# Cross attention's second half of heads is divided by its sums on POOL instead of DVE

## The reference

```python
d = Cx // H                      # 128 // 8 = 16
qh = (x @ wq.T + bq).reshape(Bx, N, H, d).transpose(0, 2, 1, 3)
kh = (memory @ wk.T + bk)...     # memory: the 154 context tokens
vh = (memory @ wv.T + bv)...
a = jax.nn.softmax(jnp.einsum('bhnd,bhmd->bhnm', qh, kh) / jnp.sqrt(jnp.float32(d)), axis=-1)
ca = jnp.einsum('bhnm,bhmd->bhnd', a, vh).transpose(0, 2, 1, 3).reshape(Bx, N, Cx)
ca = ca @ mha_out_w.T + mha_out_b
```

## Time and profile before

| | us |
|---|---|
| median of 3 runs | 882.4 |
| lowest and highest run | 880.11, 885.28 |
| the profiled execution | 884.99 |
| its span | 883.2 |
| PE busy | 727.9 |
| DVE busy | 570.5 |
| ACT busy | 534.4 |
| POOL busy | 322.5 |

### The profile page before, as it was taken

One profiled execution on the slowest core, in us unless ns is written; L12 is line 12 of the kernel. 1 busy time (PEld: TensorE's weight loads), 2 busy tenths in 40 slices (PEclk: granted clock), 3 DMA queues, 4 the chain that ended last, 5 costly groups with the idle time before them and its releaser, 6 DMA issues.

```text
span 883.2 us, 15858 instructions
## 1 busy us (share of the span) xinstructions
PE 727.9 (82%) x5368; PEld 476.9 (54%) x5368; DVE 570.5 (65%) x2212; ACT 534.4 (61%) x1345; POOL 322.5 (37%) x368
## 2 busy tenths in 40 slices
PE   5858788887878876788969789869888888879997
PEld 4535465565656745654546465545564564665443
DVE  5585856768646849658776747647567565873623
ACT  4248395684937425465696695795785845544542
POOL 4254624555341234234445425335233124412200
PEclk9598989998987977699999999999889898989999
DMA  8601010010100000202121301200212000004243
GB/s 261 192 10 34 13 43 13 13 32 13 43 13 1 1 1 1 67 16 69 37 67 37 90 19 40 75 1 20 71 26 55 18 26 30 13 13 126 72 129 91
DMA packets 37163, 41.83 MB, mean 47 GB/s; under 512 B 14346, under 2 KB 23772, under 8 KB 36956
## 3 DMA queue, kind: packets, MB, share of 16 engines
q1 hardware_dynamic: 37083, 40.83, 16.6%
HBM read 28.75 MB, written 2.62 MB: 36 GB/s over the span
## 4 chain that ended last, share of the span: by engine, by line
PE 45%; DVE 24%; ACT 18%; POOL 7%; issue 3%; DMA 1%; SPq 0%; DVEq 0%; POOLq 0%; ACTq 0%
ACT work L863 9%; PE moe_psum L624 5%; PE dve_psum L446 5%; PE act_psum L614 4%; PE act_psum L507 3%; PE dve_psum L517 3%; DVE work L1133 3%; PE act_psum L713 2%; PE act_psum L776 2%; DVE res_nrm L1111 2%; DVE stats L1101 2%; POOL rstd L1505 2%; DVE work L1156 2%; PE dve_psum L716 2%; POOL work L1522 2%
## 5 line engine op out<-in xcount | busy, mean ns | idle before, releaser
L1522 POOL TENSOR_TENSOR work<-work,rinv 128x512 f32<-128x512 f32 (+1 forms) x72 | 77.7, 1087 | 145.3 <-DVE rinv L1119 145.1
L863 ACT ACTIVATE work<-work,nbias,rnorm 128x128 f32<-128x128 f32 x256 | 122.7, 482 | 8.5 <-DVE nbias L1196 8.3
L1504 POOL TENSOR_SCALAR rstd<-mv 128x2 f32<-128x2 f32 x72 | 16.9, 235 | 161.2 <-DVE mv L1104 161.2
L446 PE MATMUL dve_psum<-wqkv,hTs 128*128 128x512 f32 x128 | 68.4, 661 | 2.0 <-ACT hTs L1010 2.0
L1562 POOL TENSOR_TENSOR hT<-hT,work 128x512 f32<-128x512 f32 x32 | 40.8, 1274 | 79.6 <-DVE work L1156 79.6
L846 ACT COPY v_loc<-act_psum 77x512 f32<-77x512 f32 (+2 forms) x72 | 41.6, 583 | 33.9 <-PE act_psum L451 16.2
L1133 DVE CUSTOM_DVE_ANT_0 work<-dve_psum,masks 128x128 f32<-128x128 f32 x256 | 58.2, 282 | 3.2 <-PE dve_psum L477 3.2
L846 ACT COPY hT<-act_psum 128x512 f32<-128x512 f32 (+1 forms) x60 | 31.2, 525 | 42.0 <-PE act_psum L507 23.0
L433 PE MATMUL act_psum<-ident,res_nrm 128*128 128x128 f32 x96 | 26.6, 372 | 36.4 <-DVE res_nrm L1111 36.3
L1505 POOL TENSOR_TENSOR rstd<-rstd,neg_half 128x2 f32<-128x2 f32 x72 | 52.3, 727 | 6.0
L1152 DVE TENSOR_TENSOR hT<-dve_psum,tab_a 128x512 f32<-128x512 f32 x32 | 22.1, 690 | 46.0 <-PE act_psum L458 29.6
(11 more groups left out here) (224 smaller groups left out, 2026.0 us busy)
## 6 DMA issues: line engine op xcount, KB each, us to landing
ahead<-cwT_dram SPq DMA_DIRECT2D x128, 64.0 KB, 2.0
v_loc<-v_loc SPq DMA_DIRECT2D x24, 256.0 KB, 3.7
kT<-cwT_dram SPq DMA_DIRECT2D x80, 64.0 KB, 2.0
qT<-cwT_dram SPq DMA_DIRECT2D x48, 64.0 KB, 2.1
wqkv<-in_wqkv_dram SPq DMA_DIRECT2D x2, 768.0 KB
res_nrm<-in_x_dram SPq DMA_DIRECT2D x4, 256.0 KB, 3.2
w_m<-in_w_m_dram SPq DMA_DIRECT2D x1, 1024.0 KB, 9.2
v_loc<-v_loc SPq DMA_DIRECT2D x8, 128.0 KB, 3.1
```

What stands on the lines that cost most here:

```text
L446: nc.tensor.matmul(bank[:], h, attn_w[:, k * INNER:(k + 1) * INNER], start=True, stop=True)\
L863: last = nc.scalar.activation(weights[:, i, :], weights[:, i, :], ACT.Exp, bias=nbias[u][:, b, i:i + 1], scale=scale_of(i), accum_out=sums ...
L1522: nc.gpsimd.tensor_tensor(some, some, by.unsqueeze(2).to_broadcast(list(some.shape)), ALU.mult).then_inc(ready[u], 1)
```

## The change

`divide` on DVE keeps the two reciprocals and loses the multiplication of the hi half, together with DVE's wait for its own reciprocals. POOL's `cross_attention_steps` calls `divide_half` a second time for each tile, for the hi half, right behind the lo half. Nothing else differs.

```diff
                     number, b = sm_cross(t), t % 2
                     invert_sums(u, number, b)
-                    dve.wait_ge(rinv_ready[u], half_done(number, 1))
-                    some = cprob[u][b][:, HALF:, :]
-                    nc.vector.tensor_tensor(some, some, rinv[u][:, b, HALF:].unsqueeze(2).to_broadcast([P, HALF, CTX]),
-                                            ALU.mult).then_inc(probs_hi_ready[u], 1)
...
                     for t in range(TILES):
                         divide_half(u, sm_cross(t), t % 2, cprob[u][t % 2], 0, probs_lo_ready)
+                        divide_half(u, sm_cross(t), t % 2, cprob[u][t % 2], 1, probs_hi_ready)
                         yield
```

## The result

| | before | after |
|---|---|---|
| median of the comparison, us (9 runs each) | 883.27 | 877.06 |
| lowest and highest run | 880.11, 888.09 | 874.60, 880.14 |
| profiled execution, its span | 884.99, 883.2 | 875.49, 873.7 |
| ratio of the times | | 0.9922, 95% interval 0.9896 to 0.9947 |

The changed kernel is faster by 0.8%, about 7 us with an interval of 4.7 to 9.2; the two medians are 6.2 apart. The forecast was 3.2. Its direction and range (873.5 to 885.0) held, and its size was about half.

The account below looks back on a forecast made before the run. The kernel was taken as a web of handovers between in-order engines, none filling the span (PE busy 82%). Gains at six chain places summed to 3.2 us, so 882.4 - 3.2 = 879.2 us, range 873.5 to 885.0.

Parts of the forecast that it names:

- The lock: Cross attention's divisions: DVE's and POOL's exclude each other on SBUF, so DVE's takes 1.85 us instead of 0.80.
- 281.52: Sample 0: DVE empties a bank earlier, so PE's 0.80 us wait ahead of line 723 goes; gain 0.80.
- the ten others: The ten of 16 DVE multiplications not on the chain: DVE has slack behind them, removal costed at nothing.
- 302.44: End of sample 0: PE starts on a hi half that now comes later; loss 0.25 us.
- 351.06 and 773.91: Samples 1 and 3: exp's bias is written earlier, though it waits under POOL's pair; gain 0.58 us each, bounds 0 and 1.07.
- 699.14 and 709.04: Sample 2: PE's wait at line 723 goes, gain 0.80 us; waits at lines 572, 1255 and 1262 go, gain 0.72.
- 761.70: Sample 3: line 1457 stands still until lo ends, then delays hi, PE losing 0.8 us; net gain taken as 0.
- The sum: Gains over the six places, 0.55 + 0.58 + 0.80 + 0.72 + 0 + 0.58 = 3.2 us.
- The whole wait goes: Rival: DVE's 1.85 us leaves the chain at all six places, or later steps tighten; 11.1 us, 871.3; chance 0.17.
- the six places: The six of 16 DVE multiplications on the chain: 281.52, 351.06, 699.14, 709.04, 761.70 and 773.91.
- Nothing is left: Rival: POOL's shadow on biases and other DVE lines, plus late hi halves, takes the gain; 881 to 882.4 us; chance 0.23.
- PE waits for hi: Rival: PE at line 572 waits 0.56 us for hi at each tile, 9.0 in all, 891.4 us; chance 0.10.

Follow-up runs that it names:

- ten: Kernel before, with the hi half moved to POOL only at the ten places not on the chain, (0, 2) included; 882.12 us, ratio 0.9997.
- six: Kernel before, with the hi half moved to POOL only at the six places where DVE's multiplication was on the chain; 876.24 us, ratio 0.9930.
- no_hi: Changed kernel with the hi half divided by nobody, PE waiting for its reciprocals alone; 874.9 us, ratio to before 0.9915.
- last_two: Kernel before, with the hi half on POOL in samples 2 and 3 only; 877.61 us, ratio 0.9952.
- first_two: Kernel before, with the hi half on POOL in samples 0 and 1 only; 875.97 us, ratio 0.9944.
- nudge: Kernel before, with DVE writing four reciprocals of sample 1's last tile four times more, same result; 887.81 against 880.74 us, ratio 1.0097.
- twice: Changed kernel with POOL multiplying the hi half twice, so that it comes later still; 884.62 us, ratio to before 1.0042.

## Why the prediction was right in direction and short in size

*The lock (right).* DVE's division took 1.85 because it stood still behind POOL. With both halves on POOL each takes 1.21, and with both on DVE 0.80.

*281.52 (right).* Forecast 0.80, measured 0.87. The wait ahead of line 723 is gone.

*291.42, one of the ten others (wrong).* "In the ten others DVE has slack behind it, and I cost its removal there at nothing." At (0, 2) it had none. The division held back the bias, ACT's exps and hT, and through them PE's transposes at 298.22. Its removal gave 1.77 us, 1.20 of them at the low clock too (ten), and none of them came from the clock alone (six). I had read the places from the chain that ended last, and there DVE's copy, which ended 0.06 later than ACT's, stood in ACT's place. This is the largest single term of the gain, and it was missing.

*302.44, the late hi half (right).* Forecast 0.25, measured 0.23 in the trace and 0.28 by no_hi. PE waited for a hi half at this one tile; two to four were forecast.

*351.06 and 773.91, the bias in POOL's shadow (right in size).* Forecast 0.58 each, measured 0.62 and 0.62. What I had assumed of where the bias gets in was not general. At 279.25, 694.20 and 768.33 it took 1.03, 1.03 and 1.14, through the start of the second division to its end. I had priced only waits up to the end of the division in front. In sample 1 such a wait at 339.29 cost 0.28.

*699.14 and 709.04 (right).* Forecast 0.80 and 0.72; measured 0.87 and 0.88 in the changed kernel, 1.74 for the sample in last_two.

*761.70 (wrong).* Forecast 0, because line 1457 would stand still behind lo and then push hi back by 0.8. It went first: with the division gone it starts straight behind the reciprocals, ahead of POOL. So lo was late, 0.44 at PE's line 572, and 0.79 by the start of line 593. With the wait at 339.29 the forecast was 1.1 us too good here. How much of the 0.79 is the late lo and how much the lower clock, at which PE transposed, is not shown.

*The sum (wrong, by two terms that were missing).* The terms of the edit come to 4.3 us against 3.2 forecast, with 1.77 at a place that had none and 1.1 lost where little was expected. The kernel gained 5.9 in the profile. The second step that failed is that the sum took every other stretch to keep its length. It did not. What is left over per stage is -0.1, +0.6, +1.4, -2.7, +0.9, -0.5, +2.0, net 1.6 for the changed kernel. That this goes with the clock and not with the moved divisions is shown for sample 3 (first_two has 2.3 us of it with before's instructions), for sample 2 (last_two has the same edits there and not the 0.9) and for the stretch from 1 to 2 (nudge has 6.3 of the other sign). In sample 1 PE's work from the transposes at 357.86 (351.01 in the changed kernel) to the end takes 5.41 us before and 4.02 after, at granted clocks of 0.64 and 0.98; that and the 0.6 between samples 0 and 1 were not tested by themselves. Why the clock falls at one instruction and not at another stays open.

*The rivals.* "The whole wait goes" forecast 11.1 us of gain, from later steps tightening; the six places gave no more than their own waits, and one of the ten others, (0, 2), gave 1.77 of its 1.85. "Nothing is left" expected the bias to cancel the gain: it stood still as feared, and cost 3.9 us of DVE's busy time, but not the two waits at line 723. "PE waits for hi" named the right place and it was as rare as forecast; twice shows that even 1.2 us more costs 0.4 in sample 2, measured against the kernels whose PE is busy there for about as long (42.2 us against 42.4).

The range held for reasons that it didn't state: a place that was missing, two losses and the clock happened to add up to a gain inside it, and that is luck. In these runs one untouched stretch alone moved by up to 6.6 us (317.24 to 323.81), so a range for such a kernel has to allow some us on either side for the clock.

## What to carry to other kernels

A place that the printed chain does not name can still set the time: where two engines end within 0.1 us of each other, the view picks one. Look at both before you cost a removal at nothing. An instruction that takes more than twice its shortest time is standing still: find which engine ends with it, and add up both engines' work at that place before moving it. Then check which instruction becomes the neighbour of the moved one: a two-input instruction that now starts 0.1 us earlier can take the lock from it. A change of a few microseconds in a kernel whose PE waits often is worth what its own rows give, plus or minus what the clock does in code that is not touched; compare stage by stage and look at PE's busy time in stretches with the same instructions before crediting a total to an edit.

## What was not expected of the hardware

- 0.5 us of delay at 360 us made the following 317.28 us 6.27 us longer, with the same instructions. The granted clock there went from 0.94 to 0.92, PE's busy time from 269.5 to 275.7.
- Behind 270 us the two profiles of each kernel agree to 0.07 us a stage, low phases of the clock included, and so do the stages that last_two and nudge share with before, on two other chips. Runs of other lengths were not profiled.
- A mean granted clock does not tell its price. Sample 3 of the changed kernel has 0.76 against 0.86 before and is 1.87 us shorter: its low phase lies where PE waits for ACT, before's lies on line 799 and the transposes behind it.
- A bias of 128x4, 0.17 us alone, took 1.03 and 1.14 us under two divisions of POOL in a row, others of the same kind 0.29 to 0.70.
- A removed DVE division gave 1.20 us where PE ran at the low clock and 1.77 where it ran at the full one, and the clock alone gave nothing: the two are not to be added up.
